# The two ends of the expert loop on TensorE: register loads moved into a shared chunk, the first expert product in bank 4, six matmuls moved into the loop's end

## What the kernel computes

```
x = x + 0.5 * ffn(layernorm(x))
x = x + attention(layernorm(x))
x = x + 0.5 * ffn(layernorm(x))

ffn(x):                                   # x: 1024 x 256
    g, u   = split(x @ shared_gate_up_w.T)        # 704 columns each
    shared = sigmoid(x @ shared_gate_w.T) * ((silu(g) * u) @ shared_down_w.T)
    probs  = softmax(x @ gate_w.T)                # 8 experts
    top_w, top_i = top_k(probs, 2); top_w /= sum(top_w)
    ge, ue = split(x @ w1[e].T)                   # 176 columns each, per expert e
    y_e    = (silu(ge) * ue) @ w2[e].T
    return sum over the two chosen e of top_w * y_e + shared
```

## Time and profile before

| what | value |
|---|---|
| median of three runs | 565.37 us |
| profiled execution, its own time | 565.4 us |
| its span, first to last instruction | 530.3 us |
| around the span | 35.1 us |
| busy: TensorE, VectorE, ScalarE, GpSimd | 96%, 67%, 52%, 51% of the span |
| mean granted TensorE clock | 0.998 of 2.4 GHz |

### The profile page before, as it was taken

The page is one execution under the profiler, slowest core; times in us unless marked ns, Lnnn a source line. Parts: engine busy times, 40 slices in busy tenths (PEclk is TensorE's granted clock), DMA queues, the critical chain, the costliest instruction groups (busy, mean ns, idle before and its releaser), DMA issues.

```text
span 530.3 us, 10757 instructions
## 1 busy us (share of the span) xinstructions
PE 509.8 (96%) x3345; PEld 453.6 (86%) x3346; DVE 353.9 (67%) x929; ACT 277.6 (52%) x815; POOL 271.2 (51%) x360
## 2 busy tenths in 40 slices
PE   8998899999899999999999999999999999899995
PEld 4787799897788898999998989989988788799985
DVE  5789766658664684775856847758558679566647
ACT  3973556532552663654636636546446465366640
POOL 1826877741664371671653726716533230877750
PEclk9999999999999999999999999999999999999999
DMA  7951233352001001001010010010001230233336
GB/s 282 386 167 41 80 101 104 104 188 72 1 21 59 1 22 59 5 23 52 20 59 0 20 59 0 21 58 20 0 1 41 79 121 1 64 106 100 101 95 232
DMA packets 20123, 39.34 MB, mean 74 GB/s; under 512 B 2944, under 2 KB 10496, under 8 KB 20096
## 3 DMA queue, kind: packets, MB, share of 16 engines
q1 hardware_dynamic: 15680, 26.92, 15.4%
q0 software_dynamic: 4416, 12.06, 7.1%
HBM read 29.80 MB, written 9.18 MB: 73 GB/s over the span
## 4 chain that ended last, share of the span: by engine, by line
PE 84%; DVE 9%; DMA 2%; ACT 2%; issue 1%; POOL 1%; SPq 0%; DVEq 0%; ACTq 0%
PE bank L187 20%; PE bank L189 19%; PE bank L188 19%; PE bank L1660 5%; PE bank L1672 4%; PE bank L1659 3%; PE bank L1701 3%; PE bank L1094 2%; DMA xn<-y_by_token 2%; PE bank L193 1%; PE bank L986 1%; PE bank L1699 1%; PE bank L194 1%; DVE x_res L945 1%; PE bank L1141 1%
## 5 line engine op out<-in xcount | busy, mean ns | idle before, releaser
L1404 POOL TENSOR_TENSOR s_a<-s_a,rr_a 128x128 f32<-128x128 f32 x64 | 25.8, 403 | 133.9 <-DVE rr_a L1521 133.1
L1454 ACT ACTIVATE s_a<-s_a,mn_a 128x128 f32<-128x128 f32 (+1 forms) x128 | 57.1, 458 | 18.6 <-DVE mn_a L1515 18.3
L541 POOL DMA_INDIRECT xn<-x_normed,tok_i_f x46 | 47.2, 1026 | 37.1 <-DVE tok_i_f L813 24.4
L187 PE MATMUL bank<-xT_h,area_h 128*128 128x512 f32 x124 | 51.3, 414 | 0.0
L1447 ACT ACTIVATE qk_a<-bank,bias_a 128x512 f32<-128x512 f32 x32 | 22.1, 690 | 50.8 <-PE bank L189 48.3
L189 PE MATMUL bank<-xT_h,area_l 128*128 128x512 f32 x124 | 48.6, 392 | 0.0
L188 PE MATMUL bank<-xT_l,area_h 128*128 128x512 f32 x124 | 48.5, 391 | 0.0
L1469 ACT ACTIVATE area_h<-bank,bias_a 128x256 fp32r<-128x256 f32 x64 | 29.1, 479 | 29.3 <-PE bank L1701 28.6
L1503 DVE TENSOR_SCALAR qk_a<-bank,bias_a 128x512 f32<-128x512 f32 x32 | 24.0, 750 | 29.9 <-PE bank L189 29.9
L1511 DVE SCALAR_TENSOR_TENSOR s_a<-bank,cst 128x384 f32<-128x384 f32 x64 | 35.2, 550 | 8.5 <-PE bank L1660 8.4
L1515 DVE TENSOR_REDUCE mn_a<-s_a 128x1 f32<-128x128 f32 (+1 forms) x128 | 39.2, 347 | 2.2
(11 more groups left out here) (207 smaller groups left out, 1698.1 us busy)
## 6 DMA issues: line engine op xcount, KB each, us to landing
area<-in_wqkv SPq DMA_DIRECT2D x8, 768.0 KB, 4.2
area_r<-in_w SPq DMA_DIRECT2D x16, 256.0 KB, 3.9
xn<-y_by_token SPq DMA_DIRECT2D x12, 256.0 KB, 3.9
w_r<-in_w SPq DMA_DIRECT2D x8, 352.0 KB, 7.5
x_normed<-xn SPq DMA_DIRECT2D x4, 512.0 KB, 4.9
area<-in_wo SPq DMA_DIRECT2D x8, 256.0 KB, 2.6
x_res<-in_x_in SPq DMA_DIRECT2D x4, 256.0 KB, 4.2
wgu_r<-in_wgu SPq DMA_DIRECT2D x4, 256.0 KB, 6.8
```

The lines of the kernel that those rows point to most:

```text
L187: pe.matmul(psum, lhs[0], rhs[0], start=first, stop=False)
L541: pool.indirect_dma_start(xe[m % XR], None, xd, bass.IndirectOffsetOnAxis(ap=tok_i[:, m:m + 1], axis=0)).then_inc(s_xe[m % XR], 16)
L1404: pool.tensor_tensor(s[b][:, 0:P], s[b][:, 0:P], rr[:, b, 0:1].to_broadcast([P, P]), ALU.mult).then_inc(s_p, 1)
L1454: act.activation(s[b][:, cols], s[b][:, cols], ACT.Exp, bias=mn[:, b, t:t + 1], scale=-1.0, accum_out=rs[:, b, t:t + 1]).then_inc(s_e, 1)
```

## The change

TensorE, before the loop: both register loads, with their wait for `s_expert`, move from behind the chunk 9 to between its two halves (`first_tile`). The four filler matmuls (`ENTRY`) go, and so do the waits for the silu of chunk 9 before up(0) and for the token list before up(1). up(0) writes bank 4 in place of bank 2; the wait for the silu now stands before up(2), the next that writes bank 2.

TensorE, at the loop's end: the gate half of chunk 10 is cut in two parts of three matmuls; one goes ahead of inner_turn(22), one ahead of down(21). The up half and chunk 11 stay behind down(22). The first down product of the second half takes its chunks in three groups.

ScalarE and VectorE: `s_up` counts halves instead of chunks. The silu of a full chunk waits for the gate half alone, the product on VectorE also for the up half. On ScalarE the silu of chunk 10 moves from behind the last eviction to ahead of the eviction of tile 21.

```diff
+                def ups(c):
+                    return 2 * (c + 1) - (c + 1) // SC
+                def gates_up(c):
+                    return ups(c) - (1 if c % SC < SC - 1 else 0)
                 def up_bank(m):
-                    return bank[5 if m == 1 else 2 + m % 2]
+                    return bank[4 + m if m < 2 else 2 + m % 2]
...
                     def shared_silu(c):
-                        act.wait_ge(s_up, c + 1)
+                        act.wait_ge(s_up, gates_up(c))
...
+                        if m == NM:
+                            shared_silu(SC + AHEAD)
                         if m >= 2:
                             tile_out(m - 2, m % 2)
...
-                    for c in range(SC + AHEAD, 2 * SC):
-                        shared_silu(c)
-                        shared_high(c)
+                    shared_high(SC + AHEAD)
+                    shared_silu(2 * SC - 1)
+                    shared_high(2 * SC - 1)
...
                     def shared_mul(c):
                         dve.wait_ge(s_silu, c + 1)
+                        dve.wait_ge(s_up, ups(c))
...
-                    def shared_up(c, between=None):
+                    def shared_part(c, g, k):
...
+                        last = split_matmuls(pe, bank[2 * (c % 2) + g][:, :],
+                                             (wgu_h[:, at:at + P], wgu_l[:, at:at + P]),
+                                             (xT_h[:, k, toks], xT_l[:, k, toks]), k == 0, k == KD - 1)
+                        if k == KD - 1:
+                            last.then_inc(s_up, 1)
+                    def shared_up(c, between=None):
+                        for g in range(2 if c % SC < SC - 1 else 1):
+                            if g and between:
+                                between()
                             for k in range(KD):
+                                shared_part(c, g, k)
...
-                        for cs in (range(SC - 1), range(SC - 1, SC)):
+                        for cs in ((range(AHEAD), range(AHEAD, SC - 1), range(SC - 1, SC)) if half and not pair
+                                   else (range(SC - 1), range(SC - 1, SC))):
...
                     def first_tile():
                         pe.wait_ge(s_silu, SC + AHEAD - 1)
                         tile_in(0, 0)
+                        pe.wait_ge(s_expert, 1)
+                        for reg in (e_up, e_turn):
+                            pe.reg_load(reg, tile_e[0:1, 0:1])
 
                     shared_up(SC + AHEAD - 1, first_tile)
                     pe.wait_ge(s_hl, SC + AHEAD - 1)
                     tile_in(1, 1)
-                    keep_warm(pe, 4, ENTRY)
-                    pe.wait_ge(s_silu, SC + AHEAD)
...
-                    pe.wait_ge(s_expert, 1)
-                    for reg in (e_up, e_turn):
-                        pe.reg_load(reg, tile_e[0:1, 0:1])
-                    up(0, 0)
+                    up(0, 0, up_bank(0))
                     next_experts(1)
                     tile_in(2, 0)
-                    pe.wait_ge(s_tok, 1)
                     up(1, 1, up_bank(1))
                     next_experts(2)
                     inner_turn(0, 0)
                     tile_in(3, 1)
+                    pe.wait_ge(s_silu, SC + AHEAD)
                     up(2, 0)
...
                     down(m - 2, 0, more=False)
                     next_experts(m)
+                    shared_part(SC + AHEAD, 0, 0)
                     inner_turn(m, 0)
+                    shared_part(SC + AHEAD, 0, 1)
                     down(m - 1, 1, more=False)
                     next_experts(m)
                     down(m, 0, more=False)
-                    for c in range(SC + AHEAD, 2 * SC):
-                        shared_up(c)
+                    for k in range(KD):
+                        shared_part(SC + AHEAD, 1, k)
+                    shared_up(2 * SC - 1)
```

More of the change, by code:

```diff
@@ L39 @@
 WARM = (24, 4, 22)
-ENTRY = 4
 STEPS = 6
@@ L908, in inner_mul @@
                                           ALU.mult).then_inc(s_em, 1)
-                    inner_mul(0, 0)
+                    inner_mul(0, 0, up_bank(0))
                     lows_of("turn0")
@@ L1010, in logits @@
                         last.then_inc(s_lgt, 1)
-                    def shared_up(c, between=None):
+                    def shared_part(c, g, k):
                         half, ch = divmod(c, SC)
-                        if first and c < SC - 1:
+                        if first and c < SC - 1 and g == 0 and k == 0:
                             pe.wait_ge(s_wh, c + 1)
                             wait_low(pe, c)
-                        toks = slice(half * HALF, (half + 1) * HALF)
-                        for g in range(2 if ch < SC - 1 else 1):
+                        if not first and c == 0 and g == 0 and k == 0:
+                            pe.wait_ge(s_ov, BATCH * NP)
+                        if c >= 2 and k == 0:
+                            if g == 0 and (c - 2) % SC < SC - 1:
+                                pe.wait_ge(s_silu, c - 1)
+                            else:
+                                pe.wait_ge(s_hl, c - 1)
+                        toks = slice(half * HALF, (half + 1) * HALF)
+                        at = ch * CH + (g * KD + k) * P
+                        last = split_matmuls(pe, bank[2 * (c % 2) + g][:, :],
[3 more added lines that the diff above has]
+                            last.then_inc(s_up, 1)
@@ L1020, in shared_up @@
+                    def shared_up(c, between=None):
+                        for g in range(2 if c % SC < SC - 1 else 1):
                             if g and between:
                                 between()
-                            if not first and c == 0 and g == 0:
-                                pe.wait_ge(s_ov, BATCH * NP)
-                            if c >= 2 and g == 0 and (c - 2) % SC < SC - 1:
-                                pe.wait_ge(s_silu, c - 1)
-                            elif c >= 2:
-                                pe.wait_ge(s_hl, c - 1)
@@ L1030, in shared_up @@
-                            for k in range(KD):
-                                at = ch * CH + (g * KD + k) * P
-                                last = split_matmuls(pe, bank[2 * (c % 2) + g][:, :],
-                                                     (wgu_h[:, at:at + P], wgu_l[:, at:at + P]),
-                                                     (xT_h[:, k, toks], xT_l[:, k, toks]), k == 0, k == KD - 1)
-                        last.then_inc(s_up, 1)
+                            for k in range(KD):
+                                shared_part(c, g, k)
```

## The result

Changed kernel: 566.91 us, median of 20 runs (562.63 to 571.98). The kernel before, in turn with it: 565.18 us, median of 20 (561.73 to 567.92). The ratio is 1.0042, with a 95% interval of 1.0023 to 1.0060: 0.4% slower, where 563.9 had been forecast, and 0.3 us above the range.

The account below looks back on a forecast made before the run. GpSimd, not TensorE, was taken to set the pace of the expert loops. Gains of 0.53 us in the first feed-forward block and 0.95 in the second made 1.48, from 565.4 to 563.9; 8-in-10 range 562.3 to 566.6.

Parts of the forecast that it names:

- the second look at the fillers: Before the first feed-forward block's transposes: idle grows from 0.36 to about 2.6 us; a clock fall would cost 2.5.
- R2: Rival: the clock falls in the gap before the first feed-forward block's transposes, 566.4 up to 567.4 us; chance 0.17.
- Entry: Start of both expert loops: up(0) comes 2.1 us earlier in the first block, 1.4 to 1.9 in the second.
- The head start inside the loop: TensorE's gain at loop entry, carried through the expert loops of both blocks: 1.8 us, range 1.4 to 2.1.
- but nearly: Inside the expert loop: TensorE does not catch up with the gathers, but nearly; gather lands 97.5, tile_in(22) at 98.3.
- Exit: End of the expert loop: moved matmuls delay the scatter chain by 0.57 us and help TensorE's own end by 0.86.
- the delay is covered, with 0.7 to spare: Loop's end: eviction 21 still ends 1.2 us earlier than before, while GpSimd would be ready 0.53 earlier.
- R3: Rival: the gain at loop entry is used up, both scatter chains 0.27 us later, 565.9; below 1.1 gain; chance 0.08.
- What bounds the kernel: Expert loops: GpSimd is full throughout, 46 issues at about 1.28 us, so TensorE's savings hardly count.
- the waits that the prediction named as the most: GpSimd's remaining waits, the most a faster TensorE can give: 0.26 us in the first block, 0.51 in the second.
- The token list's 0.27: Before each expert loop: the gate-half silu moves VectorE's token work and GpSimd's first gather 0.27 us earlier.
- VectorE does wait for the loads: End of the second block: VectorE waits for loads instead of being later; gain 0.95 us, range 0.78 to 1.6.

Follow-up runs that it names:

- E17: The changed kernel once more, unaltered, on an occasion of the quick level: 534.37 us, 1.0028 of the kernel before.
- E9: The kernel before with every tile taking expert 0, so no register loads or address work on TensorE: 534.56 us, 1.0049.
- E15: The kernel before with 2 fillers in place of 22 before the first feed-forward block's transposes, slow level: 565.47 us, 1.0051.
- E8: The kernel before with 2 fillers in place of 22 before the first feed-forward block's transposes: 565.16 us, 1.0037.
- E7: The changed kernel with ScalarE's tiles 8 to 19 of each expert loop as a hardware loop: 564.82 us, 1.0048 of the kernel before.
- E13: The changed kernel, unaltered, run again beside the kernel before at the slow level: 567.73 us, 1.0080.
- E10: The kernel before with registers loaded once and all tiles taking that expert's weights, address work kept: 533.72 us, 1.0044.
- E16: The changed kernel with the loop entry of the kernel before, run on another occasion, slow level: 567.36 us, 1.0082 of the kernel before.
- E4: The changed kernel with the loop entry of the kernel before; loop-end part and gate-half silu stay: 566.87 us, 1.0047 of the kernel before.
- E14: The changed kernel with 48 fillers in place of 22 before the first feed-forward block's transposes, slow level: 565.03 us, 1.0041 of the kernel before.
- E18: The changed kernel with 48 fillers in place of 22, at the quick level: 532.29 us, 1.0002 of the kernel before.
- E11: The changed kernel without the loop-end part and with 36 fillers in place of 22, quick level: 531.19 us, 0.9984 of the kernel before.
- E6: The kernel before with ScalarE's tiles 8 to 19 of each expert loop as a hardware loop, not straight code: 563.73 us, 1.0015.
- E5: The changed kernel with 48 fillers in place of 22 before the first feed-forward block's transposes: 562.52 us, 1.0004 of the kernel before.
- E1: The kernel before, unchanged, profiled at the slow level: 564.43 us, 1.0007.

## Why the prediction was wrong, step by step

**The step that failed is the second look at the fillers.** It found the right mechanism and the right idle (about 2.6; E17 has 2.56), and then gave it 0.17, as R2, and put nothing for it in the sum, because the clock had once fallen only four to five microseconds after the last matmul. One such fall was no bound: after the last filler it came some two microseconds later in E9 and five in the changed kernel. Every trace with an idle of 2.0 us or more before these transposes shows half clock at or behind them (2.02 E15, 2.09 E8, 2.19 E7, 2.24 E13, 2.34 E10, 2.56 E17, 2.65 E16, 3.12 E9 and the changed kernel), and none of the eleven with 1.65 (E4) or less does. In eight of these nine the clock fell only during or behind the transposes, so that the idle ahead of them was not the whole quiet stretch: eight transposes and 0.56 to 0.67 of waiting for ScalarE follow, and no other matmul.

That fits the rule of the Trainium skill that the prediction quoted ("TensorE: Matmul & The Clock Gate", Part 4), by which transposes do not count as busy in the way matmuls do. No run here tests it by itself, and in E9 it isn't needed, since there the clock fell in the idle.

The price was put at 2.5 and measured as 2.1 to 2.9 at the slow level (0.37% and 0.51% in E8 and E15, 0.39% between E13 and E14). At the quick level E17 less E18 is 1.4 by the ratios and 2.1 by the medians; there the 48 fillers overshoot and are themselves the last thing that the transposes wait for, so it is a lower figure. In the traces (of both levels), the first projection and the thirteenth matmul start 2.81 to 2.85 us apart in the eleven that kept the clock, 4.21 to 4.43 in six of the others and 5.25 or 5.26 in three: 1.4 to 2.4 us in that stretch alone.

Two things in it were luck. The 2.5 was read at the program's start, where the profile's granted clock over the first 10 us is 1.00, so no run shows that the slow fillers there are the clock's. And R2's time, 566.4 to 567.4, holds the measured 566.9, but it was built on a profile of the other level and on a gain of 1.5 that at the slow level is not there.

**Entry.** Right in place: up(0) in f0 at 53.63 in E17 (forecast 53.4), without idle. In f1 it starts 8.85 after the first gather (462.37, 453.52) and not 10.35 (461.49, 451.14): 1.5 nearer, at the low end of 1.4 to 1.9. The head start inside the loop was taken as 1.8. tile_in(4) starts 1.64 earlier in E17 (60.14 against 61.78) and tile_in(22) 1.15 (98.98 against 100.13): the head start shrinks as TensorE closes on the gathers, which the prediction named ("but nearly") and did not price.

**Exit.** The size was right: the eviction of tile 21 comes 0.59 later, in every trace of the slow level with the exit (its scatter waits 1.22 to 1.25 in both blocks) against every one without it (0.64 to 0.66); forecast 0.57. The cover, the prediction's "the delay is covered, with 0.7 to spare", was wrong. At the quick level the wait in f0 is 0.38 and in f1 0.59, where 0.30 had been forecast for both and E11, without the exit, shows it: 0.37 us in all, since the head start at the loop's end was 1.15 in f0 and 0.9 in f1 (tile_in(22) counted from the first gather: 53.67 before, 52.78 in E17) and not 1.8, about the 1.1 that R3 named as its point. At the slow level nothing covers it, because GpSimd waits for an eviction at every one of the last scatters, and 2*0.59=1.2 us show in full.

**What bounds the kernel.** For the quick level the reading was right, and E9 and E10 bear it out: with work taken from TensorE, the loops get shorter by the waits that the prediction named as the most (0.23 and 0.48 us in E9, forecast 0.26 and 0.51) and by hardly more (0.41 and 0.54 in E10). For the level at which the time was measured it holds only for part of the loop: there ScalarE's late starts lengthen both loops, GpSimd waits 0.7 to 2.4 us every two to six issues, and the last scatters come at TensorE's 2.0 to 2.2 us. The trace and the times of before did not belong together, and the sign was in the table: 35.1 us around a span of 530.3 had no row anywhere, and the prediction took it as fixed.

**Sum at the quick level.** Forecast -0.53 in f0, -0.95 in f1. From the first gather to the last scatter E17 takes 63.55 in f0 (before 63.91) and 61.25 in f1 (before 61.56): -0.36 and -0.31 instead of -0.26 and -0.51. The token list's 0.27 is there: from f0's last scatter to f1's first gather E11 takes 342.80, before 343.11. In f0 the start itself wanders (43.6 to 44.4 in unchanged code), but GpSimd's idle ahead of the first gather, counted from one earlier operation, is 11.40 or 11.41 us in all eight traces without the gate-half silu and 11.13 to 11.16 in all twelve with it: the forecast 0.27. Then DMA takes it back. In f0 the fourth load of y_by_token lands 5.51 after issue, not 5.13, and the transposes start at 122.21 against 122.25. In f1 VectorE does wait for the loads, as forecast, but the last load takes 5.99 against 4.38, and the span ends 18.4 after the start of the last scatter where before it was 17.6. The steps taken as fixed are not fixed to half a microsecond, and a gain of 1.5 was summed across two of them. E18, with the clock kept, says 1.0002: of the forecast 1.5 us about nothing. E11, without the exit, gets 0.9.

**Left open.** Why ScalarE starts late at the slow level stays open. It is not its straight code (E6), and it came with the occasion, not with the kernel; E9 and E10 were meant for it and fell on an occasion without late starts. Nor is it shown what makes up the rest of E14's 0.4%: the late evictions are 1.2 us of its 2.3, and E5, the same kernel, did not show a loss.

## What to carry to other kernels

Before working a sum on a profile, check that its span and the measured times belong to one another: a large difference between them that no row explains can mean that the profile shows another regime, with another bound. When a change makes TensorE finish earlier in front of a wait that does not move, it makes a gap, and a fall of the clock in that gap is part of the bill; fillers have to be set again with every change ahead of them, long enough to keep the clock and short enough not to be waited for. A matmul block put "into a gap" ahead of the last product on a chain delays that chain by its own length less the gap, and should go where nobody is waiting.

## What the runs showed of the hardware that was not expected

- The same program on the same chip took 532 us on one occasion and 563 on another. Of the 32.2 us between the spans of before and E1, 31.0 lie in the two expert loops (first gather to last scatter 63.91 and 61.56 us, against 78.90 and 77.53), where ScalarE starts operations 1 to 3.9 us late though their inputs are complete; from the last scatter of f0 to the first gather of f1, attention between them, the kernel before takes 343.1 us at the quick level and 343.6 at the slow one (E1).
- Idles of TensorE of 2.0 to 3.1 us ahead of eight transposes went with half clock in nine of nine traces; idles up to 1.65 us in none of eleven. The clock fell some two to five microseconds after the last filler.
- Removing work from TensorE (E8: 20 fillers; E9: all register and address work of the loops; E10: the register loads) made the kernel 0.4 to 0.5% slower.
- 256 KB loads of y_by_token took different times from issue to landing in like places: the fourth load of f1 5.17 us in E11 and 6.95 in E18, the last of f1 4.38 before and 5.99 in E17.
